# Half of the loads of x on SyncE's queue, ahead of the first table store

## The reference

```python
h   = relu(layernorm(x))
deg = segment_sum(ones, src);  dinv = where(deg > 0, rsqrt(max(deg, 1)), 0)
norm = -dinv[src] * dinv[dst]
conv(h) = h @ W0 + segment_sum(h[src] * norm, dst) @ W1 + b
h   = leaky_relu(layernorm(conv_1(h)) * gamma + beta, 0.01)
out = x + conv_2(h)
```

## Time and profile before

| | us |
|---|---|
| median of 3 runs | 2083.22 (2079.54 to 2084.0) |
| the profiled execution | 2077.38 |
| its span in the trace | 2075.6 |
| POOL busy | 1507.3 (73%) |
| PE busy | 1742.7 (84%) |
| DVE busy | 776.0 (37%) |
| ACT busy | 317.4 (15%) |
| indirect gathers at L560 (1536) | 1454.8, and 470.5 idle in front of them |

### The profile page before, as it was taken

How to read it: one execution, slowest core, us unless ns; L and a number is a source line. 1 busy time by engine, 2 the same in 40 slices (tenths; PEclk the granted TensorE clock), 3 DMA queues, 4 the chain that set the end, 5 groups by cost and what they waited for, 6 DMA issues and landing times.

```text
span 2075.6 us, 25930 instructions
## 1 busy us (share of the span) xinstructions
PE 1742.7 (84%) x8740; PEld 666.3 (32%) x8740; DVE 776.0 (37%) x2411; ACT 317.4 (15%) x647; POOL 1507.3 (73%) x1596
## 2 busy tenths in 40 slices
PE   3459888888888888888888988888898888888888
PEld 3433333332323322223333333333333333323333
DVE  9944444444454444444442222212222222222221
ACT  8701111111111111111111111000110101101010
POOL 2277777777777777777777777777777777777775
PEclk9969999999999999999999999999999999999999
DMA  9898888888888888888878888888888888888875
GB/s 262 267 328 250 244 243 242 243 241 241 236 237 241 243 241 238 237 240 241 243 228 260 256 251 256 251 255 249 253 257 248 253 254 253 256 250 256 255 242 182
DMA packets 188714, 514.94 MB, mean 248 GB/s; under 512 B 45271, under 2 KB 46958, under 8 KB 187339
## 3 DMA queue, kind: packets, MB, share of 16 engines
q0 software_dynamic: 128576, 422.78, 69.2%
q1 hardware_dynamic: 56374, 90.16, 12.5%
q10 hardware_dynamic: 3638, 0.42, 0.3%
HBM read 472.40 MB, written 40.84 MB: 247 GB/s over the span
## 4 chain that ended last, share of the span: by engine, by line
POOL 61%; issue 21%; PE 10%; DVE 6%; DMA 1%; ACT 1%; SPq 0%; DVEq 0%; ACTq 0%
POOL arena L560 61%; PE ps L1232 4%; PE ps L1356 4%; DVE w_all L844 2%; DVE work L844 1%; PE ps L1224 1%; DMA scal<-node_scales 0%; DVE ps L1101 0%; ACT arena L689 0%; DMA arena<-table,idx_all 0%; PE ps L1420 0%; DVE stats L1104 0%; DVE ps L1111 0%; DMA node_scales<-scal_all 0%; DVE stats L853 0%
## 5 line engine op out<-in xcount | busy, mean ns | idle before, releaser
L560 POOL DMA_INDIRECT arena<-table,idx_all x1536 | 1454.8, 947 | 470.5 <-issue 467.4
L1356 PE MATMUL ps<-arena,hots 128*32 128x512 f32 x5048 | 729.1, 611 | 135.6 <-DVE hots L1023 77.2
L1356 PEld LDWEIGHTS ps<-arena,hots 128*32 128x32 f32 x5048 | 186.4, 110 | 653.7 <-issue 458.1
L1023 DVE TENSOR_SCALAR hots<-iota_f,loc_all,arena 128x64 f32<-128x64 f32 (+1 forms) x768 | 234.1, 334 | 341.1 <-DMA arena<-table,idx_all 339.9
L1232 PE MATMUL ps<-arena 128*128 128x512 f32 (+1 forms) x432 | 196.6, 597 | 35.8 <-ACT arena L689 35.8
L1232 PE MATMUL ps<-w_all,arena 128*128 128x512 f32 (+1 forms) x432 | 196.1, 597 | 35.8 <-ACT arena L689 35.8
L679 ACT ACTIVATE arena<-ps,scal 128x512 f32<-128x512 f32 x106 | 73.0, 689 | 921.8 <-PE ps L1420 883.6
L1232 PE MATMUL ps<-arena,work 128*128 128x512 f32 (+1 forms) x432 | 199.5, 605 | 0.0
L1232 PE MATMUL ps<-w_all,work 128*128 128x512 f32 (+1 forms) x432 | 193.2, 591 | 0.0
L1140 DVE SCALAR_TENSOR_TENSOR ps<-ps,scal,arena 128x512 f32<-128x512 f32 x52 | 39.5, 759 | 351.1 <-PE ps L1232 351.1
L1224 PE MATMUL ps<-ident,arena 128*128 128x128 f32 x848 | 137.4, 286 | 27.7 <-DMA scal<-node_scales 20.3
(11 more groups left out here) (158 smaller groups left out, 725.9 us busy)
## 6 DMA issues: line engine op xcount, KB each, us to landing
arena<-table SPq DMA_DIRECT2D x106, 256.0 KB, 4.0
arena<-table,idx_all POOLq DMA_INDIRECT x1550, 4.0
table<-arena SPq DMA_DIRECT2D x53, 256.0 KB, 4.0
arena<-in_x_dram SPq DMA_DIRECT2D x53, 256.0 KB, 5.7
out_dram<-arena SPq DMA_DIRECT2D x53, 256.0 KB
table<-arena SPq DMA_DIRECT2D x10, 1124.4 KB
arena<-in_x_dram POOLq DMA_DIRECT2D x9, 1120.0 KB, 34.0
w_all<-in_L_gnn_W_dram SPq DMA_DIRECT2D x2, 1024.0 KB, 14.0
```

The source lines that it names most:

```text
L560: nc.gpsimd.indirect_dma_start(out=rows_of(n, c)[0:rn, 0:RW if L == 0 else D], out_offset=None, in_=table[L][0:NEAR if near else N, :], in ...
L1023: hot = nc.vector.tensor_scalar(hot_of(n, c)[:, cols], iota_f[:, cols], loc, factor_of(i, c), ALU.is_equal, ALU.mult)
L1356: return nc.tensor.matmul(tx_ps[n % 2][strip, :], hot_of(n, c)[:, strip], rows_of(n, c)[:, 0:D], start=start, stop=stop)
```

## The change

SP issues the loads of the groups 1, 3, 5, 7 and 9, right behind that of group 0 and ahead of its wait at L365 and all stores. POOL keeps the groups 2, 4, 6, 8 and 10. The semaphores, the sizes and the splitting of each load stay as they are.

```diff
             for n0, n1 in parts:
                 sp.dma_start(nodes[n0:n1, XG[0]:XG[1], :], x_rows[n0:n1, XG[0]:XG[1], :],
                              max_dma_last_dim=4 * D).then_inc(s_x[0], 16)
 
+            for g in range(1, NG, 2):
+                for n0, n1 in parts:
+                    sp.dma_start(nodes[n0:n1, XG[g]:XG[g + 1], :], x_rows[n0:n1, XG[g]:XG[g + 1], :],
+                                 max_dma_last_dim=4 * D).then_inc(s_x[g], 16)
+
...
             x_rows = x.rearrange("(p t) n -> p t n", t=NT)
-            for g in range(1, NG):
+            for g in range(2, NG, 2):
                 for n0, n1 in ((0, TA), (TA, TR)):
                     pool.dma_start(nodes[n0:n1, XG[g]:XG[g + 1], :], x_rows[n0:n1, XG[g]:XG[g + 1], :],
                                    max_dma_last_dim=4 * D).then_inc(s_x[g], 16)
```

## The result

The changed kernel takes 2090.29 us (median of 7 runs, 2087.55 to 2093.68) against 2080.71 us of the kernel before in the same series (7 runs); the ratio is 1.0045 [1.0033, 1.0056], so **9.4 us slower**. The profiled execution took 2088.5 us, its span is 2086.7 us, against 2077.38 and 2075.6 of the kernel before: 11.1 us more, profiled against profiled.

What follows compares the result with a forecast made beforehand. It took a 99.50 us start-up, then a stream of gathers paced by POOL, as the bound. Profiled 2077.38 + 0 + 3.2 = 2080.6, plus 5.84 to the median gave 2086.4, stated as 2086.0 us; range 2081.5 to 2094.

Steps and rivals of the forecast that it cites:

- Part 1 and 2: Ten load issues leave POOL, worth nothing; ten go to SP before its first store, 4 us, hidden in SP's wait.
- Part 3: Landing order of x: group 1 at 15.7 us, group 3 at 28.5; last table store 3.2 us later (1.5 to 8.3).
- rival (a): SP's queue runs at 80 to 95 GB/s beside POOL's, or stops between groups: +4.2 to +8.3 us; chance 0.25.
- The sum: Profiled 2077.38 + 0 + 3.2 = 2080.6 us; with 5.84 to the median 2086.4, stated as 2086.0.
- Part 4: Stores and ids behind SP's loads: delay hidden, zero cost, unless x is done later than 56 us.
- rival (c): Store backlog on SP: x done after 56 us, ids late or last stores queue; +4 to +8 us; chance 0.06.
- (b): SP's and ACT's DMA issues hold each other up: +9 to +15 us, 2092 to 2098; chance 0.09.
- (d): SP's and POOL's queues share evenly in bytes, 150 GB/s each, nobody late: +0, 2083.2 us; chance 0.09.
- (e): SP's queue takes most, group 2 lands near 29 us, last store 9.3 us later: 2092.5 us; chance 0.05.
- (f): Faster by over 0.2%: VectorE's steps shorten with fewer of POOL's descriptors written beside them; chance 0.04.
- The signs I named: Trace signs: VectorE idle 1 to 4 us before tile 4, group 3 starting at 27 to 33, first gather at 101 to 105.
- The last test: Gather stream: the prediction is wrong if the time between first gather and end changes.

Runs made afterwards that it cites:

- e2: Against the kernel before: group 1 alone goes to SP's queue, POOL keeps groups 2 to 10; ratio 1.0026.
- e3: Against the changed kernel: POOL waits for group 1 to land before it issues its loads; ratio 1.0045.
- e1: Against the changed kernel: group 1 goes back to the head of POOL's queue, SP keeps 3, 5, 7, 9; ratio 1.0003.
- e4: Against the changed kernel: all ten groups on SP's queue in order, POOL issues none; ratio 1.0027.
- e6: Against the kernel before: SP waits for the last group of x to land before its first store; ratio 1.0066.
- e9: Against the kernel before: last table store split, tiles 45 to 48 stored when ScalarE is done, only tile 49 waits for VectorE; ratio 1.0000.
- e7: Against the kernel before: SP waits for group 7 of x to land before its first store; ratio 1.0009.

## Why the prediction was right, and where it was not

**What bounds the kernel**: right in the main. In all ten kernels the median time follows the first gather to within 2 us (changed: +8.6 at the gather, +9.4 in time). That sets many executions beside the gather of a single one. In the profiled executions themselves, the stretch from the first gather to the end of the span is 1976.1 us before, 1978.6 changed, and from 1975.3 (e2) to 1984.3 (e3) in the others, so it is not as fixed as the prediction had it.

**Part 1 and 2, the issues**: right that they are worth nothing by themselves. SP was stopped inside them, as the earlier trace rows had hinted: 13.8 us at most, and that is not what cost the time in the changed kernel: in e1 the first store left later still, at 39.59, and no loss can be told.

**Part 3, the order of landing**: the mechanism was right in each of its steps up to the last store, the size of one term was not. The step that failed is "what both move together, I take 300 GB/s". Three views tell what loads of x move (first q1 alone in e4, from 28 to 34 us, then q0 alone in e6, from 40 to 46 us; both together in the changed kernel above; packets, MB, share of 16 engines):

```profile
q1 hardware_dynamic: 718, 1.40, 105.0%
```

```profile
q0 software_dynamic: 380, 1.32, 105.2%
```

1.40 MB in 6 us is 233 GB/s, 1.32 is 220, and both queues together moved 1.39 in 6 us, 232. So in these windows the rate is that of these loads, whoever issues them, and a second queue adds nothing. The Trainium skill's rule that spreading DMAs over SP, ACT and GpSimd doesn't help the bandwidth (DMA: Bandwidth & Descriptors, section Rules for kernel authors) agrees with these three figures. The 328 GB/s that drew my number up is of a single microsecond, from 4 to 5 us, with group 0 on q1 (its 0.29 MB are in the earlier trace rows, q0 added 0.04). Group 0 is a load of x too, so that microsecond is not typical even of these loads: from 5 to 12 us the two queues of the changed kernel moved 1.83 MB, 261 GB/s, and 232 from 12 us on. Why the first microseconds are faster is not shown. The lower end of the bounds, 240 together and 80 for SP, was the right one: measured 77, 90 and 82 (0.74 MB in 9 us to 33 us). Group 1 was late by the same terms: q1 had moved its 1.68 MB by about 15.5 us instead of 13.2, and it was there at 18.38 instead of 15.7, past the upper bound of 17.6. Group 3's position came at 30.3 us instead of 26.0, and it landed 3.2 us behind it instead of 2.5; together the 5 us between 28.5 and 33.48. That makes ScalarE 11.4 us late instead of 6.4 and the store 8.6 instead of 3.2: the upper bound, +8.3, plus 0.3. It is rival (a), which had 0.25, and the forecast of "inside 0.2%" that had 0.42 fell with the term.

**The sum**: the time of 2090.29 is inside the range, but that the 2086.4 of the sum came as near to it was partly luck. From one profiled execution to the other the sum had +3.2 us, at most +8.3; measured are +11.1, of which 8.6 lie in front of the first gather and 2.5 behind it, where the prediction had nothing. The 5.84 us that it added from the profiled execution to the median were 1.79 in the changed kernel, and this hid 4.0 of the 7.9 us of the miss. By the medians of one series the loss is 9.4 us, three times what the sum had.

**Part 4, stores and ids behind the loads**: "zero" came true, but with less room than the text gave it. x was not done at 49 us but only near 57, q1's stores and ids then moved 8.07 MB from 60 to 84 us, 336 GB/s instead of 385, and the source ids landed at 69.3, not 59. It was past the 56 us named as the tipping point, and still cost nothing at the gather: TensorE turned the ids at 77.09. The late engines were not all that hid it: in e1 ScalarE was done at 94.44, 7.5 us sooner than in the changed kernel, with x done near 57 as well, and 6.15 us lay between it and the first gather as ever. e4, where the first store leaves 10 us later than in e1 and x is done near 60 us, loses 5.5 us by its stores. Where all groups come in order on SP, rival (c) takes the place of (a): that is e4.

**Rivals (b), (d), (e), (f)**: (b) fell by ScalarE's nearly unchanged issues, and q1's loads were never held: it passed as many packets as q0 in each window from 12 to 30 us; (d) and (e) fell by the even packet counts, with 1.8 to 2.1 KB a packet on q1 and 3.2 to 3.7 on q0; (f): VectorE's steps are the same 2.23 us.

**The signs I named**: VectorE's stall was to be 1 to 4 us and is 4.35; group 3 was to start at 27 to 33 and starts at 33.48; ScalarE ends last; the first gather was to be at 101 to 105 and is at 108.11. The test "first gather moves by ScalarE's last ReLU less 3.2 us" holds: 11.85 - 3.2 = 8.65, measured 8.61. The last test failed: the time from first gather to the end grew by 2.5 us in the profiled execution. POOL waited that long at the first gather that needs the factors (timeline of the changed kernel):

```profile
128.03 0.94 POOL L565 DMA_INDIRECT arena<-table,idx_all  x1 [2.49 <-DMA table<-factors]
```

In the other kernels this wait is 0 to 4.1 us. In e1 it is 0.3, as before, and the stretch behind the first gather is 3.9 us longer than before all the same, so the wait is not the whole of the spread. The stores of the factors are issued 0.25 us ahead of the first gather in all kernels but e9, and POOL goes on at most 18.2 us after their issue in the kernel before, 20.2 in the changed one, 21.8 in e3. What makes them longer in one execution than in another, none of these runs tells; it stays open.

## What to carry to other kernels

Before moving a load to a second queue, ask in which order its rows are wanted and what will stand beside it: two full queues passed equal numbers of packets here, so the queue with the smaller packets got the smaller share, and the transfer that had been first in the one queue came 4.7 us after it was wanted. If the engines are already full of one kind of load, a second queue changes only the order, so price it with the rate that this kind of load holds over several microseconds, not with the best microsecond in the trace. And give a landing time a range: the same group in the same place came up to 2.7 us apart. And ask what else sits in the queue that gets the loads: here stores that began 24 us late cost nothing at the first gather, 28 us late behind all loads cost 5.5, and 44 us late cost 14.

## What the hardware did that I had not expected

- One issue on SP's queue held the engine for 13.8 us while its queue was full of loads. Everything behind it in SP's program waits as well.
- Loads of 2 KB rows into 125 partitions moved 220 to 233 GB/s in the windows of 6 us shown above, from either queue or both, while q1 with the stores moved 331 (e4, 84 to 100 us, 8.3 KB a packet) to 390 (2.34 MB in 6 us from 60 us on in the changed kernel). Why the loads stop there was not tried.
- POOL's cast of the source ids took 2.03 us in the changed kernel, where it fell beside one of VectorE's count steps, which took 1.52 us instead of 0.98. The same cast took 1.15 us before, 0.82 in e6, where VectorE stood still for it, and 3.78 in e7. The longer step is the 0.5 us by which VectorE ended later (5.25 us) than it started on tile 4 (4.68 us) (timeline of the changed kernel):

```profile
70.68 1.52 DVE L849 TENSOR_TENSOR work<-sel,work 125x1600 bf16<-125x1600 bf16 x1
```
